# First batch of a selective-scan block: two of four block-diagonals built by VectorE, cube and du moved to it, and a new order of all work

## What is computed

```python
x = jnp.einsum('bld,ed->bel', hidden_states, in_proj_w)
...
dt = jax.nn.softplus(dt + dt_proj_b[None, :, None])
A = -jnp.exp(A_log)
...
def step(state, inp):
    d, b, c, u = inp
    dA = jnp.exp(d[..., None] * A)
    state = state * dA + (d * u)[..., None] * b[:, None, :]
    y = jnp.einsum('bdn,bn->bd', state, c)
...
y = y + D[None, :, None] * x
y = y * silu(z)
...
x = x + jnp.tanh(g_xattn[0]) * _L0_xattn_ref(ctx_1024, _layernorm(x, axis=-1), ...)
x = x + jnp.tanh(g_ffn[0]) * _L0_ffn_ref(_layernorm(x, axis=-1), ...)
```

## Time and profile before

| | |
|---|---|
| median of 3 runs | 190.58 us (190.2 to 190.88) |
| the profiled execution | 192.25 us |
| its span | 190.4 us |
| TensorE, matmuls | 174.0 us busy, 91% |
| VectorE | 160.5 us, 84% |
| ScalarE | 152.7 us, 80% |
| GpSimd | 124.0 us, 65% |
| DMA | 24.59 MB, 129 GB/s in the mean |

### The profile page before, as it was taken

How to read it: one execution, slowest core, us unless ns; L and a number is a source line. 1 busy time by engine, 2 the same in 40 slices (tenths; PEclk the granted TensorE clock), 3 DMA queues, 4 the chain that set the end, 5 groups by cost and what they waited for, 6 DMA issues and landing times.

```text
span 190.4 us, 3401 instructions
## 1 busy us (share of the span) xinstructions
PE 174.0 (91%) x1098; PEld 139.4 (73%) x1098; DVE 160.5 (84%) x263; ACT 152.7 (80%) x388; POOL 124.0 (65%) x88
## 2 busy tenths in 40 slices
PE   2997528999999999999998999999999999989994
PEld 1794417879978987977796887785966586778783
DVE  0599660899999999999989999999999998996462
ACT  3347995959999999998999899899996897655630
POOL 3000476577599999829998659899994996440000
PEclk9999965899999999999999999999999999999999
DMA  5999169916898711268300474819037000001011
GB/s 125 329 390 278 2 160 300 398 37 28 136 384 235 288 41 2 9 191 261 104 0 0 103 130 51 281 40 296 0 106 280 3 0 0 0 5 57 0 57 57
DMA packets 32530, 24.59 MB, mean 129 GB/s; under 512 B 19344, under 2 KB 25216, under 8 KB 32512
## 3 DMA queue, kind: packets, MB, share of 16 engines
q1 hardware_dynamic: 31968, 24.36, 45.3%
q10 hardware_dynamic: 544, 0.01, 0.2%
HBM read 21.08 MB, written 3.28 MB: 128 GB/s over the span
## 4 chain that ended last, share of the span: by engine, by line
PE 62%; POOL 12%; DVE 8%; issue 8%; ACT 6%; DMA 1%; POOLq 0%
PE m_ps L1057 22%; PE w_ps L1111 10%; PE y_ps L1081 10%; PE w_ps L1128 7%; POOL hb L409 6%; PE w_ps L1119 3%; PE w_ps L1034 2%; ACT dA L689 2%; PE y_ps L1069 2%; DVE xc L815 2%; PE y_ps L987 2%; POOL gw L424 2%; PE w_ps L1026 1%; DVE xstat L856 1%; POOL u L392 1%
## 5 line engine op out<-in xcount | busy, mean ns | idle before, releaser
L409 POOL TENSOR_TENSOR hb<-hb,cs 128x1024 f32<-128x1024 f32 x31 | 73.9, 2406 | 8.4 <-DVE hb L891 5.1
L891 DVE TENSOR_TENSOR_SCAN hb<-dA,m_ps 128x1024 f32<-128x1024 f32 x30 | 67.6, 2273 | 6.5 <-PE m_ps L1057 6.4
L1057 PE MATMUL m_ps<-bd,duT 128*128 128x256 f32 (+1 forms) x216 | 58.6, 416 | 1.7 <-ACT duT L704 1.2
L689 ACT ACTIVATE dA<-dt,nega 128x255 f32<-128x255 f32 (+1 forms) x144 | 54.8, 461 | 0.0
L1057 PEld LDWEIGHTS m_ps<-bd,duT 128*128 128x128 f32 x216 | 40.4, 196 | 11.9 <-issue 4.8
L1081 PE MATMUL y_ps<-identf,hb 128*128 128x128 f32 x256 | 31.5, 273 | 0.0
L1081 PEld LDWEIGHTS y_ps<-identf,hb 128*128 128x128 f32 x256 | 29.0, 141 | 2.2 <-issue 1.6
L1111 PE MATMUL w_ps<-w13T,xqT 128*128 128x352 bf16 x192 | 30.4, 313 | 0.0
L1111 PEld LDWEIGHTS w_ps<-w13T,xqT 128*128 128x128 bf16 x192 | 18.5, 98 | 9.7 <-issue 0.4
L1128 PE MATMUL w_ps<-w2T,iqT 128*128 128x256 bf16 x144 | 16.5, 273 | 0.0
L424 POOL TENSOR_TENSOR gw<-gg,normw 128x704 f32<-128x704 f32 x7 | 12.6, 1795 | 5.0 <-DVE gg L933 5.0
(11 more groups left out here) (140 smaller groups left out, 268.6 us busy)
## 6 DMA issues: line engine op xcount, KB each, us to landing
cs<-c_rows SPq DMA_DIRECT2D x16, 512.0 KB, 6.2
bd<-b_diag SPq DMA_DIRECT2D x14, 512.0 KB, 6.5
b_diag<-zeros SPq DMA_DIRECT2D x1, 2048.0 KB, 9.2
gw<-in_L_ffn_w SPq DMA_DIRECT2D x1, 1408.0 KB, 8.9
x<-in_x SPq DMA_DIRECT2D x1, 1024.0 KB, 6.6
out<-ctx_in SPq DMA_DIRECT2D x8, 128.0 KB, 1.7
ru<-in_L_ffn_w SPq DMA_DIRECT2D x1, 704.0 KB, 10.7
bd<-b_rows SPq DMA_DIRECT2D x2, 256.0 KB, 3.6
```

What stands on the lines that cost most here:

```text
L409: E.tensor_tensor(h_g, h_g, cs[:, s0:s0 + sn, l0:l0 + ln], ALU.mult).then_inc(hc_end if (b, i, h) == OUT_END else hc_ok[h], 1)
L689: last = act_fn(dA_g[:, s, 1:ln], dt[:, p, h, l0 + 1:l0 + ln], ACT.Exp, scale=nega[:, h, s0 + s:s0 + s + 1])
L891: V.tensor_tensor_scan(hb[:, k % 3, h], dA[:, k % 2, h].rearrange("p n l -> p (n l)"), m_ps[:, h], 0.0, ALU.mult, ALU.add).then_inc(scan_o ...
L1057: last = T.matmul(m_q[:, :, c * P - l0:(c + 1) * P - l0], duT[:, p, c, h * P:(h + 1) * P], bd[:, (s0 + sn // 2 * q) // GN, c, n0:n0 + sn / ...
```

## The change

For the first batch, quarters 0 and 1 of `bd` no longer come through DRAM. Two new steps make each: bT (TensorE) multiplies `low` by four columns of the identity, once per half of the tokens, which puts B with tokens on the partitions into a bank of PSUM; bd (VectorE) multiplies the identity, repeated for eight (half, state) pairs, by those columns, in one tensor_tensor of 1024 columns. bput/0 writes eight rows in place of sixteen, and bget/0.0 and bget/0.1 are gone. The first batch's cubic and du, two halves each, go from GpSimd to VectorE. WARM has 6, 10 and 10 transposes in its last three pieces in place of 8 each. And the lists of all five engines are new from start to end; what each step does is otherwise the same.

```diff
@@ -28,7 +28,7 @@
 LN_CLIP = math.log(1e-5 / 127.0)
 BANK = 512
 NWORK = 3
-WARM = (8, 10, 8, 8, 8, 8, 8, 8)
+WARM = (8, 10, 8, 8, 8, 6, 10, 10)
 NWP = 9
 CROW, BROW = 32, 64
 PM = (None, None, None, 1)
@@ -70,7 +70,7 @@
 
 def diagonals(b, g):
 
-    return sum(1 for a in range(b + 1) if a == BATCH - 1 or not by_pool(a, g))
+    return sum(1 for a in range(0 if g >= NG // 2 else 1, b + 1) if a == BATCH - 1 or not by_pool(a, g))
 
 
...
-        ctxT/0.0 winT/0.0 inproj/0.0 ctxT/1.0 inproj/0.1 warm/0.0 warm/0.1 xpwT/0.0 dtwT/0.0 warm/0.2 warm/0.3
...
+        ctxT/0.0 winT/0.0 inproj/0.0 inproj/0.1 warm/0.0 dtwT/0.0 warm/0.1 xpwT/0.0 warm/0.2 xdbl/0.0 ctxT/1.0
+        dtproj/0.0 bT/0.0 warm/0.3 w/0.0 dtproj/0.1 w/0.1 warm/0.4 w/0.2 inproj/1.0 duT/0.0 warm/0.5 w/0.3 warm/0.6
...
+        winT/0.0 conv/0.0 conv/0.1 clamp/0.0 dtwT/0.0 clamp/0.1 xstat/0.0 u/0.0 u/0.1 xstat/1.0 lowc/0.0 xstat/2.0
+        xstat/3.0 bd/0.0 series/0.0 cubic/0.0 w_res/0.0 dt/0.0 w_res/0.1 series/0.1 du/0.0 cubic/0.1 w_res/0.2
+        dt/0.1 conv/1.0 w_res/0.3 du/0.1 bd/0.1 clamp/1.0 gates/0.0 scan0/0.0 scan1/0.0 w_res/0.4 lowc/1.0 scan0/0.1
...
-        cubic/0.0 dtadd/0.0 cubic/0.1 du/0.0 dtadd/0.1 du/0.1 u/1.0 w_lo/0.0 diag/0.0 w_lo/0.1 out0/0.0 w_lo/0.2
...
+        dtadd/0.0 dtadd/0.1 w_lo/0.0 w_lo/0.1 diag/0.0 u/1.0 w_lo/0.2 out0/0.0 out1/0.0 w_lo/0.3 out0/0.1 sz/0.0
...
-        l_ctx/0.0 l_x/0.0 l_xpw/0.0 l_g/0.0 l_dtw/0.0 zero/0.0 l_dtb/0.0 l_alog/0.0 l_w13/0.0 l_d/0.0 cput/0.0
...
+        l_ctx/0.0 l_dtw/0.0 l_g/0.0 l_alog/0.0 l_x/0.0 l_d/0.0 l_dtb/0.0 l_xpw/0.0 l_w13/0.0 zero/0.0 l_w2/0.0
...
     "ctxT": [("ctxT", "act")], "inproj": [("conv", "dve")], "xdbl": [("lowc", "dve")], "dtproj": [("absx", "act")],
-    "duT": [("duT", "act")],
+    "bT": [("bd", "dve")], "duT": [("duT", "act")],
     "szT": [("szT", "act")], "xqT": [("xqT", "act")], "up": [("relu", "act"), ("gate", "dve")],
...
@@ -454,8 +455,9 @@
                             if diagonals(b - 1, g):
                                 sp.wait_ge(b_got[g], 16 * diagonals(b - 1, g))
                     with nc.allow_non_contiguous_dma("one element of the diagonal per token and state"):
+                        s0 = NS // 2 if b == 0 else 0
                         for c in range(HALVES):
-                            sp.dma_start(d_diag[:, c, :], low[BROW:BROW + NS, p, c * P:(c + 1) * P]).then_inc(b_put, 16)
+                            sp.dma_start(d_diag[s0:NS, c, :], low[BROW + s0:BROW + NS, p, c * P:(c + 1) * P]).then_inc(b_put, 16)
...
@@ -833,6 +835,12 @@
                             dve.wait_ge(b_row[b - 2], 16)
                         dve.wait_ge(b_put, 16 * HALVES * (b - 1))
                     V.tensor_copy(low[:, p], bank("xdbl", b, i)[0:LOWC, 0:L]).then_inc(free["dve"], 1)
+                elif name == "bd":
+                    dve.wait_ge(work_full, full("bT", b, i))
+                    V.tensor_tensor(bd[:, i], identf[:, :].unsqueeze(1).unsqueeze(1).broadcast_to([P, HALVES, GN, P]),
+                                    bank("bT", b, i)[:, 0:HALVES * GN].rearrange("p (c n) -> p c n", c=HALVES)
+                                    .unsqueeze(3).broadcast_to([P, HALVES, GN, P]),
+                                    ALU.mult).then_inc(free["dve"], 1)
...
@@ -1033,6 +1041,13 @@
                     for j, h in enumerate(halves(b, i)):
                         last = T.matmul(ps[:, j * L:(j + 1) * L], dtwT[:, h * P:(h + 1) * P], low[0:RANK, p], start=True, stop=True)
                     last.then_inc(work_full, 1)
+                elif name == "bT":
+                    pe.wait_ge(free["dve"], emptied("xdbl", b, 0))
+                    ps = claim(name, b, i)
+                    for c in range(HALVES):
+                        last = T.matmul(ps[:, c * GN:(c + 1) * GN], low[:, p, c * P:(c + 1) * P],
+                                        identf[0:LOWC, BROW + GN * i:BROW + GN * (i + 1)], start=True, stop=True)
+                    last.then_inc(work_full, 1)
...
@@ -1051,7 +1066,10 @@
                     for c in range(l0 // P, (l0 + ln) // P):
                         for q in range(2):
                             g = (s0 + sn // 2 * q) // GN
-                            pe.wait_ge(b_got[g], 16 * diagonals(b, g))
+                            if b == 0 and g < NG // 2:
+                                pe.wait_ge(free["dve"], emptied("bT", b, g))
+                            else:
+                                pe.wait_ge(b_got[g], 16 * diagonals(b, g))
                             m_q = states(m_ps[:, h, q * BANK:(q + 1) * BANK], b, i)
                             n0 = (s0 + sn // 2 * q) % GN
                             last = T.matmul(m_q[:, :, c * P - l0:(c + 1) * P - l0], duT[:, p, c, h * P:(h + 1) * P],
```

More of the change, by code:

```diff
@@ L93 @@
[L93 to L97, removed]
@@ L117 @@
+        xqT/2.0 relu/2.0 decay0/3.3 relu/2.1 decay1/3.3 iqT/1.1 center/3.0 relu/2.2 rs1/3.0 relu/2.3 square/2.0
+        xqT/3.0 square/2.1 relu/3.0 rs2/2.0 relu/3.1 square/3.0 rs1/3.1 center/3.1 rs2/3.0 iqT/2.0 iqT/2.1 iqT/3.0
+        xqT/3.1 relu/3.2 relu/3.3 square/3.1 rs2/3.1 iqT/3.1
     """,
     "dve": """
-        winT/0.0 conv/0.0 conv/0.1 xstat/0.0 clamp/0.0 xstat/1.0 clamp/0.1 u/0.0 xstat/2.0 u/0.1 xstat/3.0 lowc/0.0
-        dtwT/0.0 gates/0.0 conv/1.0 series/0.0 clamp/1.0 dt/0.0 series/0.1 w_res/0.0 dt/0.1 w_res/0.1 w_res/0.2
@@ L121 @@
-        scan0/0.0 lowc/1.0 w_res/0.3 scan1/0.0 scan0/0.1 scan1/0.1 conv/2.0 series/1.0 cubic/1.0 dt/1.0 scan0/0.2
-        du/1.0 w_res/0.4 scan1/0.2 w_res/0.5 clamp/2.0 scan0/0.3 scan1/0.3 w_res/0.6 scan0/1.0 scan1/1.0 yz/0.0
-        w_res/0.7 x1/0.0 scan0/1.1 scan1/1.1 lowc/2.0 w_res/0.8 scan0/1.2 conv/3.0 absx1/0.0 quant1/0.0 series/2.0
-        cubic/2.0 dt/2.0 scan1/1.2 gate/0.0 gate/0.1 du/2.0 scan0/1.3 scan1/1.3 gate/0.2 absmax/0.0 clamp/3.0
-        scan0/2.0 gate/0.3 yz/1.0 x1/1.0 absmax/0.1 scan1/2.0 scale2/0.0 absx1/1.0 lowc/3.0 scan0/2.1 outscale/0.0
@@ new lines @@
+        conv/2.0 scan1/0.1 series/1.0 cubic/1.0 dt/1.0 scan0/0.2 w_res/0.5 scan1/0.2 w_res/0.6 du/1.0 scan0/0.3
+        clamp/2.0 scan1/0.3 scan0/1.0 scan1/1.0 yz/0.0 w_res/0.7 x1/0.0 scan0/1.1 lowc/2.0 w_res/0.8 scan1/1.1
+        scan0/1.2 conv/3.0 absx1/0.0 quant1/0.0 series/2.0 cubic/2.0 dt/2.0 scan1/1.2 gate/0.0 du/2.0 scan0/1.3
+        clamp/3.0 gate/0.1 gate/0.2 scan1/1.3 gate/0.3 absmax/0.0 scan0/2.0 yz/1.0 absmax/0.1 x1/1.0 scan1/2.0
+        scale2/0.0 lowc/3.0 scan0/2.1 absx1/1.0 outscale/0.0 quant1/1.0 scan1/2.1 series/3.0 quant2/0.0 gate/1.0
@@ L141 @@
+        sz/1.0 w_lo/0.6 out1/1.1 w_lo/0.7 w_lo/0.8 dtadd/2.0 out0/1.2 out1/1.2 out0/1.3 gated/0.0 out1/1.3 gated/0.1
+        sz/2.0 u/3.0 out0/2.0 out1/2.0 sz/3.0 out0/2.1 cubic/3.0 out1/2.1 out0/2.2 dtadd/3.0 gated/1.0 du/3.0
+        out1/2.2 gated/1.1 out0/2.3 out1/2.3 pm0/3.1 out0/3.0 pm1/3.1 out1/3.0 out0/3.1 out1/3.1 out0/3.2 gated/2.0
+        out1/3.2 gated/2.1 out0/3.3 gated/3.0
     """,
     "sp": """
-        l_ctx/0.0 l_x/0.0 l_xpw/0.0 l_g/0.0 l_dtw/0.0 zero/0.0 l_dtb/0.0 l_alog/0.0 l_w13/0.0 l_d/0.0 cput/0.0
```

71 lines of the change are left out of this document (34 added, 37 removed).

## The result

The changed kernel took 189.22 us (median of 6 runs, 188.7 to 189.66), the kernel before 191.19 us (median of 6 runs beside it, 190.2 to 194.48). The ratio is 0.9887, 95% interval [0.9846, 0.9928]: faster by 1.1%, some 2.15 us, where 2.7 were forecast. In absolute time the forecast was 187.9 us, counted from the earlier median of 190.58. The profiled execution took 189.44 us, span 187.6 (before: 192.25 and 190.4).

What follows compares the result with a forecast made beforehand. No one engine bounded it: a slow start, then a full stretch. The first scan 2.3 us earlier, a lead of 2.7 us at scan0/1.0 carried to the end, took 190.58 to 187.9 us; range 185.8 to 190.7.

Steps and rivals of the forecast that it cites:

- Part 1: Start up to the copy of low: xdbl at 12.8 us, copy ended at 14.2, dtproj about 1.3 us earlier.
- TensorE's queue then decides: Before xdbl: TensorE's warm and small transposes, ending near 11.8 us, then warm/0.2, set xdbl's start at 12.8.
- first rival: Start: x_proj's weights land too late, behind D and the bias; -2.0 to +4.6 us, middle 191.9 us; chance 0.13.
- signs of being wrong: VectorE or TensorE waiting for a load before 13 us, bd over 2 us, clock at 0.5, or first scan alone on time.
- Part 2: VectorE's queue from the copy of low: 16.4 us of work, first scan at 30.6 against 32.94, 2.3 us earlier.
- the two removed reads of the scratch cost nothing on the path: SP's work at the start: two reads removed at no path cost; the kept ones late only if landing after about 44.
- Part 3: Before the first scan: nothing arrives later than 30.6 us; mix0/0.0 from about 24.9 to 26.8, or 28.7 at low clock.
- the clock is no term of the sum: First mix, TensorE: it ends before the first scan at 30.6 us at either clock, 26.8 or 28.7.
- Part 4: First scan to the end: scan0/1.0 at 58.7 us against 61.45, a lead of 2.7 us, kept.
- in the full part nothing is taken away, so I carry it to the end: Full stretch and tail: the 2.7 us lead at scan0/1.0 stays whole to the end of the span.
- second rival: Full stretch, 60 to 160 us: the lead is absorbed, 0 to 0.6 us left, 190.3 us; chance 0.12.
- rule against the change: Cubes and du on VectorE: shared-port exclusion with GpSimd, up to 1.2 us at du/0.1, making the sum -1.5.

Runs made afterwards that it cites:

- e12_all_xpw: Changed kernel with batch 3's reads ahead of store/0.0, out0/3.1 held back, new tail order, earlier cget/0.3, x_proj's weights right behind x; 0.9849 of the kernel before.
- e3_old_loads: Changed kernel with SP's first ten loads in the old order, zeros ahead of the bias, A_log, w13 and D; ratio to the kernel before 0.9972.
- e4_few_warm: Changed kernel without the 50 transposes of warm/0.3 to warm/0.7, whose results nobody reads; ratio to the kernel before 0.9844.
- e7_tail_order: Changed kernel with another order of VectorE, TensorE and ScalarE work in the tail alone; ratio to the kernel before 0.981, median 188.85 us.
- e6_sp_order: Changed kernel with SP issuing batch 3's last reads of diagonals and C rows ahead of store/0.0; ratio to the kernel before 1.0083.
- e10_port: Changed kernel with batch 3's last reads ahead of store/0.0 and GpSimd's out0/3.1 waiting for VectorE's quant1/2.0; ratio to the kernel before 0.9942.

## Why the prediction was right, and where it was not

**Part 1 held in its times, in part by luck.** xdbl at 12.93 (12.8), the copy of low ended at 14.41 (14.2). But "TensorE's queue then decides" is not what the trace shows. The second group of warm transposes took 1.26 us for 10, not 0.22 each, so the queue was through at 10.27, and then TensorE waited 1.52 us for the weights of x_proj, to 11.78: two errors that cancelled. This wait is the first rival's, and was on the prediction's list of signs of being wrong. It stayed small, as D and the bias held SP for 0.58 and 0.47 us and not for the 3.62 and 1.83 of the earlier trace rows; with the zeros out of the way the landing was before the 14.2 us from which it would have decided. In e12_all_xpw, where nothing waits for these weights, xdbl starts at 12.30, so the wait is worth 0.6 us at most.

**Part 2 held in its prices and was 1.3 us long in its sum.** bd took 1.22 and 1.21 (1.25), the cubes 0.43 and 0.42, du 0.42 and 0.48. The queue took 15.14 us, not 16.4. The busy times of rows were added up, but the next instruction starts a little before the end of one: w_res is busy for 0.69 us at 18.51 and the next starts at 19.11, 0.60 later. The 33 rows from the first xstat to the last of gates add up to 16.2 us of busy time, close to the count of 16.4, and fill 15.2 us of time.

**What Part 2 didn't see is what the zeros held up.** It took w13 as there. e3_old_loads shows that with the zeros ahead of it TensorE waits 2.64 us for it once low is early. The step "the two removed reads of the scratch cost nothing on the path" left out what hung on them: that the zeros may move back behind w13 once the first scan needs no read is worth 1.6 us (0.0085).

**Part 3 held.** mix0/0.0 at 24.18 to 26.07 (24.9 to 26.8), clock 1.00; and e4_few_warm bears out "the clock is no term of the sum" with the clock at 0.83, to within 0.35 us at the first scan. At 0.50 over the whole stretch, as before, it wasn't tried.

**Part 4 failed twice, and the errors cancelled.** The lead at scan0/1.0 was 5.5 us, not 2.7. Of the 2.8 us more, 1.1 stood at the first scan already (29.55, not 30.6), 1.2 were added up to dt of batch 1, which ended at 44.73 and not at 47.0 (0.4 of that is the hold by ScalarE that did not come, the rest mostly rows that overlap as in part 2), and 0.5 from there on. The text had kept such a lead for its low end, with the gap between the first two scans of before as its reason. And the step "in the full part nothing is taken away, so I carry it to the end" is the one that was wrong: of 5.5 us 2.7 were given back, 0.5 by 80 us, 0.8 in batch 3 up to the last scan, 1.4 behind it. The last 1.4 are 0.7 from the last scan to the last sums and 0.7 from there to the end, where the stretch grew from 22.5 us to 23.2. e7_tail_order brings that stretch to 22.0, so the lost 0.7 lie in the tail's order. e6_sp_order and e10_port show that the wait for the C rows in batch 3 can't be taken away for nothing. The second rival, a lead that is absorbed, was half right: its mechanism, with half its size. What takes the 0.5 us before 80 us, the 0.8 in batch 3 and the 0.7 between the last scan and the last sums, stays open: no run took one of them back. That the forecast of 2.7 us came near the gain is therefore luck in its size; the cause of the earlier start is as it was forecast.

**The rule against the change** (the shared port) cost next to nothing where it was expected, at du/0.1: it took 0.48 us where du/0.0 took 0.42, since the w_lo operation beside it (24.09 to 26.37) ended 0.19 us after its start. It decided in batch 3 of e6_sp_order and e10_port, which the prediction did not consider.

## What to carry to other kernels

When a transfer leaves the critical path, ask what else its place forced: here the zeros ahead of w13. Carry a lead to the end step by step, through the last waits and the tail's order. Before taking a wait away, look at what the other engine does in that time: an idle GpSimd can be what lets VectorE run. And when a forecast time is met, check that the step it was added up from is the one that the trace shows: xdbl was on time here although its queue was 1.5 us early and a load 1.5 us late.
